# First attention: row maxima from the high parts alone, one row tile of TensorE a head, three maxima in a row

## What is computed

```
def L0_xattn(q, k, v, mask, Wq, bq, Wk, bk, Wv, bv, Wo, bo):      # q = layernorm(x), k = v = ctx
    qh, kh, vh = project and split into 16 heads of 16
    attn = einsum('bhqd,bhkd->bhqk', qh, kh) * 16 ** -0.5
    attn = where(mask, -inf, attn)
    attn = softmax(attn, axis=-1)
    return (attn @ vh) @ Wo.T + bo                                # x = x + this
```

## Time and profile before

| | us |
|---|---|
| median of 3 runs | 1706.09 |
| lowest, highest | 1702.1, 1711.71 |
| profiled execution, its time | 1709.27 |
| profiled execution, its span | 1707.6 |
| first attention in it | 0 to about 430 |

### The profile page before, as it was taken

How to read it: one execution, slowest core, us unless ns; L and a number is a source line. 1 busy time by engine, 2 the same in 40 slices (tenths; PEclk the granted TensorE clock), 3 DMA queues, 4 the chain that set the end, 5 groups by cost and what they waited for, 6 DMA issues and landing times. The chain is left out here.

```text
span 1707.6 us, 18955 instructions
## 1 busy us (share of the span) xinstructions
PE 1480.1 (87%) x6061; PEld 881.2 (52%) x6088; DVE 904.5 (53%) x1684; ACT 494.4 (29%) x618; POOL 451.0 (26%) x257
## 2 busy tenths in 40 slices
PE   5899898998719889874799999999999999976886
PEld 2334343443618777752444446444644465435775
DVE  5666666765420000015467664766576656736666
ACT  2443334444102222210133332333233323320221
POOL 2000000000240000022144442544344534552333
PEclk8999999999559999995799999999999999986998
DMA  6522113220374545335456555565356655302001
GB/s 157 140 38 37 32 19 50 37 38 1 130 247 144 180 155 182 135 64 90 81 74 87 74 79 69 76 86 69 43 74 86 82 67 68 44 0 102 1 0 50
DMA packets 62238, 136.14 MB, mean 80 GB/s; under 512 B 10593, under 2 KB 21217, under 8 KB 57569
## 3 DMA queue, kind: packets, MB, share of 16 engines
q1 hardware_dynamic: 59440, 127.26, 39.5%
q0 software_dynamic: 2736, 8.13, 1.4%
HBM read 58.55 MB, written 12.06 MB: 41 GB/s over the span
## 5 line engine op out<-in xcount | busy, mean ns | idle before, releaser
L1070 POOL TENSOR_TENSOR a_probs<-a_probs 128x1024 f32<-128x1024 f32 x128 | 304.2, 2376 | 415.6 <-PE a_p_os L1633 415.1
L1141 ACT ACTIVATE a_probs<-a_p_s 128x1024 f32<-128x1024 f32 x160 | 163.7, 1023 | 378.9 <-PE a_p_s L1619 378.9
L1352 DVE TENSOR_REDUCE a_max_ctx<-a_p_m 128x1 f32<-128x512 f32 x256 | 169.9, 688 | 79.8 <-PE a_p_m L1594 76.7
L424 DVE CUSTOM_DVE_ANT_0 a_scratch<-a_p_m,a_bias_q 128x512 bf16<-128x512 f32 x256 | 163.1, 687 | 80.6 <-PE a_p_m L579 80.5
L334 ACT ACTIVATE a_probs<-a_p_s 128x1024 f32<-128x1024 f32 x128 | 130.5, 1024 | 140.8 <-PE a_p_s L604 135.9
L579 PE MATMUL a_p_m<-a_k_stack,a_q_stack 127*128 127x512 f32 x256 | 128.0, 543 | 14.5 <-DVE a_mx L424 7.0
L1633 PE MATMUL a_p_os<-a_probs,a_v 128*64 128x512 f32 x512 | 138.1, 618 | 0.0
L1514 PE MATMUL a_p_s<-a_o_raw,a_w 128*128 128x256 f32 x480 | 123.8, 392 | 13.8 <-DVE a_o_raw L1283 13.8
L1594 PE MATMUL a_p_m<-a_k_hl,a_q_hh 128*128 128x512 f32 x256 | 111.0, 481 | 18.6 <-DVE a_v L1330 8.2
L1288 DVE TENSOR_TENSOR a_yb<-a_p_os,a_yb 128x512 f32<-128x512 f32 x15 | 10.4, 692 | 218.9 <-PE a_p_os L1523 218.9
L1523 PE MATMUL a_p_os<-a_w,a_probs 128*128 128x256 f32 x480 | 118.6, 380 | 0.6 <-ACT a_probs L1118 0.6
(11 more groups left out here) (200 smaller groups left out, 2162.0 us busy)
## 6 DMA issues: line engine op xcount, KB each, us to landing
a_w<-in_L_w SPq DMA_DIRECT2D x30, 1024.0 KB, 8.0
a_q_hh<-a_hi SPq DMA_DIRECT2D x64, 256.0 KB, 5.6
a_k_hl<-a_hi SPq DMA_DIRECT2D x32, 256.0 KB, 8.0
a_k_hl<-a_lo SPq DMA_DIRECT2D x32, 256.0 KB, 9.5
a_k_h<-a_hi SPq DMA_DIRECT2D x32, 256.0 KB, 10.6
a_q_lm<-a_lo SPq DMA_DIRECT2D x32, 256.0 KB, 7.1
a_ctx_t<-in_ctx_t SPq DMA_DIRECT2D x8, 512.0 KB, 5.7
a_q_stack<-a_hi SPq DMA_DIRECT2D x32, 128.0 KB, 3.9
```

The costliest lines, as they stand in the source:

```text
L424: dve.tensor_tensor_reduce(scratch[:, fill.n % M_BANKS, :], m, bias_q[:, i % NT, :], 1.0, -3.0e38, ALU.add, ALU.max, mx[:, i:i + 1]).then_ ...
L1070: pool.tensor_tensor(probs[:, kt], probs[:, kt - 1], probs[:, kt], ALU.add)\
L1141: act.activation(probs[:, kt, :, :], p_s[:, (KT1 * p + kt) % 2, :, :], ACT.Exp).then_inc(exp_done.sem, 1)
L1352: dve.tensor_reduce(max_ctx[:, NT * head + t:NT * head + t + 1], m, AX, ALU.max)\
```

## The change

Four things change, all in the first attention.

- The maxima are taken from the high parts alone: hi times hi over 16 rows of the array instead of 127. Head i of a group has its own row tile, rows 32i to 32i + 15, and the 16 maxima of a group go round the four heads (head i % 4, query tile i // 4) instead of finishing one head first. They are still 256 matmuls of 512 columns. The value that is subtracted in the exponent is so the maximum of less precise scores.
- The stacks are laid out anew: hi of head i at rows 32i in both stacks, and at rows 16 to 31 and 48 to 63 (hi, lo in `q_stack` and lo, hi in `k_stack`). Each filling is four DMAs of 32 KB (one head each) and two of 128 KB a stack, 12 instead of 6; `LANDED` is the count that the waits now use. The scores still contract over all rows.
- In `STEPS` the parts 1 to 5 now have both scores first and then three maxima in a row, with `times_v` behind the maxima in parts 2 and 4. Before, the maxima stood ahead of, between and behind the scores, with `times_v` ahead of the last.
- In part 7 `sums` stands behind the two scores instead of ahead of them.

A step `early` is defined but stands in no row of `STEPS`, and `EARLY` is 0: it does nothing.

```diff
-                 ("key", "maximum", "score", "maximum", "score", "maximum"),
-                 ("maximum", "score", "maximum", "score", "times_v", "maximum"),
-                 ("maximum", "score", "maximum", "score", "maximum"),
-                 ("maximum", "score", "maximum", "score", "times_v", "maximum"),
-                 ("maximum", "score", "maximum", "score", "maximum"),
+                 ("key", "score", "score", "maximum", "maximum", "maximum"),
+                 ("score", "score", "maximum", "maximum", "maximum", "times_v"),
+                 ("score", "score", "maximum", "maximum", "maximum"),
+                 ("score", "score", "maximum", "maximum", "maximum", "times_v"),
+                 ("score", "score", "maximum", "maximum", "maximum"),
                  ("score", "score", "turn", "times_v"),
-                 ("sums", "score", "score", "rows"))
+                 ("score", "score", "sums", "rows"))
...
+            def fill(n, at, rows, landed):
+
+                stack, parts = ((q_stack, (hi, lo)), (k_stack, (lo, hi)))[n]
+                for i in range(G0):
+                    sp.dma_start(stack[32 * i:32 * i + DH0, at + i, :].bitcast(F32),
+                                 hi[rows + i:rows + P // 2:G0, n, :].bitcast(F32)).then_inc(landed, 16)
+                for k, part in zip((1, 3), parts):
+                    sp.dma_start(stack[DH0 * k:DH0 * (k + 1), at:at + G0, :].bitcast(F32),
+                                 part[rows:rows + P // 2, n, :].bitcast(F32)).then_inc(landed, 16)
...
             def maximum(b, fill, i):
                 m = fill.bank()
                 m_full.wait_apart(dve, b, fill.n, prep, 5)
-                dve.tensor_tensor_reduce(scratch[:, fill.n % M_BANKS, :], m, bias_q[:, i % NT, :], 1.0, -3.0e38, ALU.add,
-                                         ALU.max, mx[:, i:i + 1]).then_inc(m_free.sem, 1)
+                h, t = i % G0, i // G0
+                dve.tensor_tensor_reduce(scratch[:, fill.n % M_BANKS, :], m, bias_q[:, t, :], 1.0, -3.0e38, ALU.add,
+                                         ALU.max, mx[:, NT * h + t:NT * h + t + 1]).then_inc(m_free.sem, 1)
...
             def maximum(b, banks, g, i):
 
-                h, t = G0 * (g % NG0) + i // NT, i % NT
+                tile, t = i % G0, i // G0
+                h, rows = G0 * (g % NG0) + tile, slice(32 * tile, 32 * tile + DH0)
                 m = banks.free()
                 if i == 0:
-                    stacked[g % 2].wait(pe, b, 16 * 6 * (g // 2 + 1))
-                done(pe.matmul(m, q_stack[0:MAX_ROW, h, P * t:P * (t + 1)], k_stack[0:MAX_ROW, h, :],
-                               start=True, stop=True))
+                    stacked[g % 2].wait(pe, b, LANDED * (g // 2 + 1))
+                done(pe.matmul(m, q_stack[rows, h, P * t:P * (t + 1)], k_stack[rows, h, :], start=True, stop=True))
```

More of the change, by code:

```diff
@@ L160, in steps @@
                     continue
+                if what == "early" and g + 2 >= NG0 and not ahead:
+                    continue
                 yield what
-        FILLS = {"query": 1, "key": 1, "maximum": 1, "turn": 1, "rows": NT, "sums": 1}
-        DVE_FILLS = {"maximum": 1, "rows": NT, "sums": 1}
+        FILLS = {"query": 1, "key": 1, "maximum": 1, "early": 1, "turn": 1, "rows": NT, "sums": 1}
+        DVE_FILLS = {"maximum": 1, "early": 1, "rows": NT, "sums": 1}
         def fills(kinds, last_g=NG0 - 1):
             return sum(kinds.get(w, 0) for g in range(last_g + 1) for j in range(PARTS) for w in steps(g, j, True))
-        BEFORE = NT + 2 + 2 + N_MAX + 1
-        DVE_BEFORE = NT + 2 + N_MAX
+        BEFORE = NT + 2 + 2 + N_MAX + 1 + EARLY
+        DVE_BEFORE = NT + 2 + N_MAX + EARLY
         AT_END = 2 + 1 + NT // 2
         assert (fills(FILLS) + AT_END) % M_BANKS == 0
+        LANDED = 16 * 2 * (G0 + 2)
         x_in, weights_in, loaded = sem("x_in"), sem("weights_in"), sem("loaded")
@@ L187, in attention0 @@
         split_ready = Count(sem("split_ready"), 4)
[L188 removed]
+        stacked = [Count(sem("stacked_first"), 2 * LANDED), Count(sem("stacked_last"), 2 * LANDED)]
         mx_ready = Count(sem("mx_ready"), NG0)
@@ L321, in project @@
                 for count in stacked:
-                    count.wait(act, b, 16 * 6 * half)
+                    count.wait(act, b, LANDED * half)
                 at = half % 2
@@ L416, in split @@
                     for count in stacked:
-                        count.wait(dve, b, 16 * 6 * half)
+                        count.wait(dve, b, LANDED * half)
                 dve.tensor_tensor(lo[:, n, :], full[:, n, :], hi[:, n, :].bitcast(F32),
@@ L447, in turn @@
                 for g in range(NG0):
-                    i = 0
+                    i, early = EARLY, 0
                     for j in range(PARTS):
@@ L454, in turn @@
                                 i += 1
+                            elif what == "early":
+                                maximum(b, fill, early)
+                                early += 1
                             elif what == "turn":
@@ L512, in _ @@
             turn_maxima(-1, fill, NG0)
+            for i in range(EARLY):
+                maximum(-1, fill, i)
             dve.wait_ge(x_in, 16 * B)
@@ L633, in turn @@
                                 i += 1
+                            elif what == "early":
+                                maximum(b, banks, g + 2, early)
+                                early += 1
                             elif what == "turn":
@@ L675, in _ @@
             turn_maxima(-1, banks, NG0)
+            for i in range(EARLY):
+                maximum(-1, banks, NG0 + 1, i)
             with pe.Fori(0, B - 1) as b:
```

16 lines of the change are left out of this document (5 added, 11 removed).

## The result

| | us |
|---|---|
| before, median of 4 runs (lowest, highest) | 1708.90 (1702.1, 1711.88) |
| changed, median of 4 runs (lowest, highest) | 1742.37 (1741.22, 1757.15) |
| ratio, 95% interval | 1.0218, 1.0163 to 1.0274 |
| changed, profiled execution: time, span | 1757.15, 1755.5 |

The changed kernel is slower by 33 us; 1732 was forecast. The profiled execution was its longest, and why it was is part of the story.

The account below looks back on a forecast made before the run. TensorE was taken to bound the pair of parts (4.42 of 4.60 us), with the order of reaching three PSUM banks decisive. 19 + 4.3 + 3 = 26 us gave 1735 profiled, 1732 as median; own range 1723 to 1746, widened to 1710 to 1762.

Parts of the forecast that it names:

- The pair: Two parts, one with `times_v`: TensorE waits for the third bank until 2.62 us, then 2.56 more; 5.18 us instead of 4.60.
- The groups: Groups of four heads: groups 0 and 2 +1.0 each, group 1 +0.7 (last turn +1.9), group 3 +2.3 us.
- the sum of 26: Whole execution: 19 for three full turns, 4.3 for the last, 3 for the prologue; 1735 us profiled.
- `sums`: Part 7, `sums` behind two scores: reciprocal 1.14 us later; turned rows from group 1 to 2 +1.1 us.
- The stacks: Stack fillings, 12 DMAs instead of 6: +3 us in the prologue (0 to 3.6), 0 in the turns.
- The switch: Whole array to row tiles and back: 0.09 us each; at 0, 7 us less, at three times, 13 more.
- the first rival: First attention: TensorE's clock falls to 1.2 GHz for a third of 30 pairs, +25 us, 1757; chance 0.12.
- a cold pair: A pair of parts at 1.2 GHz: work behind the third maximum doubles but for latencies, about +2.5 us.
- The second rival: Row tiles pay if the third bank doesn't hold TensorE up: pair some 4.0 us, 1691 in all; chance 0.06.
- The third rival: Loss smaller: split groups come out even, only `sums` and prologue left, 10 us at most, 1712; chance 0.14.

Follow-up runs that it names:

- Half reads: Changed kernel with VectorE reading 256 of the 512 columns of every maximum: 1699.82 us; the same edit on the kernel before: 1687.53 us.
- the run without long falls: Changed kernel timed again with no edit (median 1746.18 us); this is its execution of 1736.95 us, at a mean granted clock of 0.932.
- the order alone: Kernel before with the new STEPS, keeping maxima over 127 rows and the old stacks: 1723.49 us, ratio 1.0076.
- the tiles alone: Changed kernel (16-row tiles, new stacks) with the steps of the kernel before: 1752.24 us, ratio 1.0251.
- two and two with row tiles: Changed kernel with no more than two maxima in a row and `sums` ahead of the scores: 1727.45 us, ratio 1.0095.
- two and two: Kernel before (127 rows, old stacks) with steps of two maxima, two scores and, in parts with `times_v`, two more maxima: 1698.28 us, ratio 0.9927.

## Why the prediction was right, and where it was not

- **The pair.** 5.18 us was worked out from the latencies of VectorE, 5.16 and 5.18 measured; the third bank free 2.62 after the first maximum, 2.61 measured; VectorE idle 1.5 us, 1.41 measured. Half reads take the wait away, and of the 42 us that go with it some 20 go in the changed kernel alone. The prediction's sentence that TensorE is the bound of the pair (4.42 of 4.60) holds for group 3; in groups 0 and 2 a pair took 5.20 before, with VectorE's splits in it.
- **The groups**, in the profile without the long falls (1736.95 us): group 1 of the second turn 19.3 us, forecast 19.2; group 3 20.22, forecast 20.4; the last two full turns 7.0 and 6.6 us longer, forecast 6.3. Other terms were off, and nearly cancel: the first turn is 7.6 us longer (from 40.45 to 126.82 before, from 42.58 to 136.56 now), the last 6.9 up to its last transpose of maxima where 1.0 + 1.9 + 2.1 = 5.0 was forecast (that sum also took 2.1 for the 2.3 of its own text), the prologue 2.1 instead of 3, and the rest of the execution is 2.5 us shorter instead of 0.7 (spans of 1735.3 and 1707.6). Against the 1708.9 of these runs the sum of 26 gives 1735, and the run without long falls took 1737. That it came so close is in part luck.
- **`sums`.** 1.1 for the rows and about as much in group 3 make 2.2 a full turn. The runs give 6.6 us in all, from 1723.49 to 1716.84. In group 3 the place is 0.7 (19.83 us with the order alone, 19.13 with `sums` first), and three in a row are the other 1.0 over the 18.15 of before. The reciprocal starts 3.29 us after the transpose instead of 2.37, 0.9 later where 1.14 was forecast.
- **The stacks.** Forecast +3 at the start, nothing in the turns. Measured about 2 us, and 1725.73 against 1723.49 leaves nothing for the turns.
- **The switch.** I took 0.09 us from the earlier trace rows, and into the 16 rows it was that: 410.96 is 0.32 after the mask matmul's load at 410.64, 0.23 and 0.09. The way out is in the 0.34 that I gave the third maximum before `times_v`. For three together that is right: from the third maximum to `times_v` it is 0.43 (408.41 to 408.84), 0.34 and 0.09. That an isolated maximum takes the same 0.43 us was no term of this sum, but it sank my own expectation for the tiles alone.
- **How the loss is made up.** By the prediction's own count 26 us were 3 for the stacks, 7 for the switches (what falls away at 0 each) and so 16 for the order. The runs without long falls give 2, 11 (1736.95 against 1725.73) and 15. The mechanism was right, and its division nearly so; the switches were priced too low.
- **The step that failed is the first rival.** I gave the fall of the clock a chance of 0.12, as a case apart at 1757 us, and wrote that scores and `times_v` would fill the pair nearly and the clock would rise again. Instead it comes in degrees, by execution: 1737 at a mean granted clock of 0.932, 1742 in the median at 0.925 and 0.926, 1757 with three groups at 1.2 GHz (0.914). My price for a cold pair (+2.5) measured +2.4. The median lies 10 us over the 1732: about 5 are this clock, which the forecast held at nothing, 3 are the kernel before, at 1709 in these runs and 1706 in the ones that I started from, and 2 the sum. The Trainium skill (TensorE: Matmul & The Clock Gate, "A second HAM failure mode: psum-queue depth-cycling") tells of a kernel whose clock oscillated because of short idle times between groups of matmuls cycling through PSUM banks. The changed kernel agrees, with 0.50 from 128 to 144 us behind such a wait. The order alone does not: it has the same stop of 0.43 us at the same bank, and with 127 rows no fall of its clock comes amid maxima.
- **The second rival**, row tiles that pay, did not come true, as its condition did not: 16 rows one behind another (1743.46) cost as much as three tiles side by side (1742.37). With short reads a pair takes 4.36 us instead of the 4.0 that I gave this rival, and full rows do as well (8.51 and 8.50 for two pairs). The Trainium skill (TensorE: Matmul & The Clock Gate, Part 3) is right that tiles overlap: three took 0.43 us here and three in one tile 0.89. The Trainium skill (TensorEngine Tiling, Key Properties) says that a change of the tiling mode drains the engine. No row shows a drain as such; that one maximum and one head's scores take 1.09 us with 16 rows and 0.69 with 127 agrees with it.
- **The third rival** has a slip: 3 x 2.3 + 3 = 10 us over 1706 make 1716, not 1712.

The loss of 33 us by the runs: three in a row 7, `sums` 7, stacks 2, 16-row maxima 17. Of these 17 some 11 are in the run without long falls (1736.95 against 1725.73), both with a clock of 0.95 over the first 440 us; the rest is the clock. These are differences between medians of separate groups of runs, good to a microsecond or two. What stays open is why few rows let the clock fall. The number of rows, exposed weight loads and changes of mode went together in every kernel with a fall amid maxima, and no run here parts them. They are not enough by themselves, as with short reads all but one fall were gone. Nor does it take three maxima in a row: the row tiles alone and two and two with row tiles had falls as well.

## What to carry to other kernels

Before grouping matmuls, count the banks they write and ask when the consumer frees the last one: an engine that works in order stops there with all that stands behind. Small matmuls in row tiles save time among their own kind; between full-array matmuls they pay the way in and out each time, and here what they saved was hidden behind a full bank. Steps that alternate two and two fitted three banks better than one and one or three in a row, so try the order by itself before the new layout. And look where the pair that you reason from is short: here the 4.60 us of group 3 stood beside 5.20 in groups 0 and 2, and the gain of two and two lay outside group 3.

## What the runs showed of the hardware

- A change between 127 or 128 rows and 16 rows exposes the weight load: 0.43 us for one 16-row maximum between two scores, 0.23 for one of 127 rows, and 0.43 for three in three row tiles.
- The mean granted clock of the same kernel went from 0.911 to 0.932 from one execution to the next, and the time from 1761.21 to 1736.95 with it. The two kernels with the new order and full rows (1723.49 and 1725.73) repeated within 3 us.
- TensorE's granted clock fell to 0.50 amid maxima only where these had 16 rows (in each of those seven profiles, with half reads for a single window of 4 us). In the seven with full rows it fell only where no maximum runs: behind the reciprocals, as in the earlier trace rows, and between two turns.
